# A gated decoder pair on one core: the feed-forward's down projection in three reduced products, the keys stacked in two parts, and a weight sum moved into the channel attention

## What is computed

```python
x = x + tanh(g_xattn[0]) * L0_xattn(layernorm(x), ctx, ctx)   # channel attention, sigmoid scores
x = x + tanh(g_ffn[0]) * L0_ffn(layernorm(x), ...)
x = x + tanh(g_xattn[1]) * L1_xattn(layernorm(x), ctx, mask, ...)  # 16 heads, 8-bit linears
x = x + tanh(g_ffn[1]) * L1_ffn(layernorm(x), W1, W2)         # ternary weights

def L0_ffn(x, w_r, b_r, w1, b1, w2, b2):
    scores = x @ w_r + b_r
    _, idx = top_k(scores, 0.5 * 512 -> k rows per batch)      # the best half, 256 tokens
    h = gelu(x[idx] @ w1 + b1)                                 # 512 -> 2048
    out[idx] = h @ w2 + b2                                     # 2048 -> 512, zero elsewhere

def weight_quant(w):                                           # of L1_ffn, W1 and W2
    scale = 1.0 / clip(mean(abs(w)), 1e-5)
    return clip(round(w * scale), -1, 1) / scale
```

## Time and profile before

| what | value |
|---|---|
| time, median of 3 runs | 994.96 us (993.64 to 995.98) |
| the profiled execution, its own time | 996.59 us |
| its span in the trace | 994.8 us |
| PE busy, share of the span | 893.2 us, 90% |
| DVE busy | 678.7 us, 68% |
| ACT busy | 573.3 us, 58% |
| mean granted TensorE clock | 0.978 of full speed |

### The profile page before, as it was taken

One profiled execution on the slowest core, in us unless ns is written; L12 is line 12 of the kernel. 1 busy time (PEld: TensorE's weight loads), 2 busy tenths in 40 slices (PEclk: granted clock), 3 DMA queues, 4 the chain that ended last, 5 costly groups with the idle time before them and its releaser, 6 DMA issues.

```text
span 994.8 us, 15838 instructions
## 1 busy us (share of the span) xinstructions
PE 893.2 (90%) x5584; PEld 585.3 (59%) x5592; DVE 678.7 (68%) x1893; ACT 573.3 (58%) x1098; POOL 81.9 (8%) x101
## 2 busy tenths in 40 slices
PE   3989998999999978699899999899999899899677
PEld 2868775576776654466544567544566545566333
DVE  5896762525222054599788699788699788699793
ACT  4546333445555133488638688548688548688443
POOL 2000203022120002400010000010000010000000
PEclk9999999999999989799999999999999999999879
DMA  5444556533351056910159310159410159300001
GB/s 190 131 166 135 193 218 232 176 129 128 103 194 43 1 169 148 192 43 2 44 107 199 118 43 2 44 108 192 124 43 2 43 108 198 118 1 2 1 1 43
DMA packets 52271, 102.83 MB, mean 103 GB/s; under 512 B 8925, under 2 KB 8925, under 8 KB 50657
## 3 DMA queue, kind: packets, MB, share of 16 engines
q1 hardware_dynamic: 39872, 71.88, 27.4%
q10 hardware_dynamic: 8160, 17.31, 5.2%
q0 software_dynamic: 4160, 12.62, 4.0%
HBM read 55.62 MB, written 14.75 MB: 71 GB/s over the span
## 4 chain that ended last, share of the span: by engine, by line
PE 39%; DVE 7%; issue 6%; ACT 6%; SPq 3%; DMA 3%; POOL 1%; ACTq 0%; DVEq 0%; POOLq 0%
PE psum L1518 8%; PE psum L1486 6%; PE psum L1535 5%; PE psum L1591 5%; PE psum L1561 5%; ACT probs L1334 3%; SPq L1187 3%; PE psum L1453 3%; DMA k<-k_lo 2%; PE psum L1463 2%; PE psum L1577 1%; PE psum L1544 1%; POOL q L1171 1%; DMA q<-first_parts 1%; PE psum L1479 1%
## 5 line engine op out<-in xcount | busy, mean ns | idle before, releaser
L1334 ACT ACTIVATE probs<-psum,neg_max 128x512 f32<-128x512 f32 x256 | 174.7, 691 | 47.3 <-DVE neg_max L1802 47.1
L1802 DVE CUSTOM_DVE_ANT_0 psum<-psum,m_in 128x512 f32<-128x512 f32 x256 | 174.3, 705 | 22.2 <-issue 22.1
L1518 PE MATMUL psum<-ident,probs 128*128 128x128 f32 x1024 | 154.0, 275 | 0.0
L1486 PE MATMUL psum<-k,q 128*128 128x512 f32 x256 | 125.4, 495 | 15.7 <-ACT probs L1334 7.3
L1518 PEld LDWEIGHTS psum<-ident,probs 128*128 128x128 f32 x1024 | 127.7, 141 | 19.6 <-issue 2.0
L674 PE MATMUL psum<-w_sb,hT 128*128 128x512 f32 x256 | 117.3, 603 | 5.9 <-ACT hT L566 5.9
L1832 DVE COPY probsT<-psum 128x512 f32<-128x512 f32 x128 | 88.1, 688 | 4.1 <-PE psum L1518 2.8
L1325 ACT COPY probsT<-psum 128x512 f32<-128x512 f32 x128 | 75.2, 588 | 20.9 <-PE psum L1518 20.9
L594 PE MATMUL psum<-xselT_hi,w_hi 128*128 128x256 f32 x256 | 81.8, 320 | 1.6 <-ACT xselT_hi L501 1.6
L1486 PEld LDWEIGHTS psum<-k,q 128*128 128x128 f32 x256 | 49.0, 192 | 53.1 <-ACT probs L1334 33.4
L674 PEld LDWEIGHTS psum<-w_sb,hT 128*128 128x128 f32 x256 | 46.9, 192 | 55.6 <-issue 48.2
(11 more groups left out here) (237 smaller groups left out, 1524.1 us busy)
## 6 DMA issues: line engine op xcount, KB each, us to landing
bw_raw<-in_L_ffn_W_dram ACTq DMA_DIRECT2D x16, 1024.0 KB, 5.4
c_in<-in_ctx_dram SPq DMA_DIRECT2D x8, 1024.0 KB, 5.3
k<-k_hi SPq DMA_DIRECT2D x24, 256.0 KB, 6.0
k<-k_lo SPq DMA_DIRECT2D x24, 256.0 KB, 6.8
q<-q_hi SPq DMA_DIRECT2D x48, 128.0 KB, 3.4
q<-q_lo SPq DMA_DIRECT2D x48, 128.0 KB, 2.5
xres<-in_x_dram SPq DMA_DIRECT2D x4, 1024.0 KB, 5.9
w_raw<-in_L_ffn_w_dram POOLq DMA_DIRECT2D x4, 1024.0 KB, 5.3
```

The source lines that it names most:

```text
L1334: act.activation(probs[:, u % 4, :], psum[u % SCORE_BANKS][:, :], ACT.Exp, scale=-1.0, bias=neg_max[:, u:u + 1], accum_out=prob_sum[:, nt, ...
L1486: pe.matmul(psum[u % SCORE_BANKS][:, :], q4[:, h, nt * P:(nt + 1) * P], k4[:, h, :], start=True, stop=True).then_inc(score_psum, 1)
L1518: mm = pe.transpose(turn_bank(u)[:, l * P:(l + 1) * P], probs[:, u % 4, l * P:(l + 1) * P], ident[:, :])
L1802: dve.tensor_tensor_reduce(bank[:, :], bank[:, :], m_in[:, nt, :], -1.0, LOWEST, ALU.add, ALU.min, neg_max[:, u:u + 1]).then_inc(masked_re ...
```

## The change

- The down projection uses `three` on high and low parts: 12 fp32r matmuls of 512 columns a pair in place of 4 fp32 ones. ACT adds a copy to `h_hi` per pair (`hidden_high`), DVE a subtraction to `h_lo` (`hidden_low`), in a ring of 3 buffers. `down(g)` runs two pairs behind `up`.
- `w2` is no longer resident as fp32. Its high part stays (`w2_hi`, made by ACT in the first 8 pairs and ahead of them). The raw rows go through a ring of 3 pair buffers, and every pair of every batch is loaded again (32 loads of 512 KB on SP) for DVE to make `w2_lo`. A slot is loaded again when `down` of three pairs before has been done.
- The ring lies on `xres` slots 1 and 2. So the order of batches is 0, 3, 1, 2 (`ORDER`): 3 is still in memory, 1 and 2 are read back from DRAM by SP (`load_x1`).
- The sums of magnitudes move into the channel attention: 3, 3 and 2 chunks at the end of batches 0, 1, 2 on ACT, ahead of the copies to `w1_hi`, through two buffers (`load_sum`) on the upper half of `w1_hi`. `FIRST_TURN` goes from 11 to 8, and the scales of both weights are made on DVE in the third pair.
- `load_selected` moves from SP to POOL. Ranks are made in two steps, in pairs 3 and 4; `route_norm` and `scores` in pairs 0 and 1, and the result of a batch is added in pair 1 of the next.
- The last `put_back` moves from the end of the first block to the head of the second. The rounding of wq and wo is spread over the pairs of the last batch; wk and wv are waited for in `layer1`.
- Keys of batches 1 to 3 are stacked in two halves (32 DMAs of 128 KB), the first as soon as two key tiles have both parts.

The core of the diff, left out lines marked:

```diff
+        RING = 3
+        ORDER = [0] + [B - 1] + list(range(1, B - 1))
...
+        w2_hi = at("w2_hi", [P, FT, C], F32R, w2_at)
+        w2_raw = at("w2_raw", [P, 2 * RING, C], F32, sh.front + 8 * K)
+        w2_lo = at("w2_lo", [P, 2 * RING, C], F32R, sh.front + 8 * K)
...
+                def load_selected(k):
+                    pool.wait_ge(xn_sel_stored, 16 * T * (k + 1))
+                    if k >= 1:
+                        pool.wait_ge(xsel_psum, 2 * k)
+                        pool.wait_ge(ids_ready, k)
+                    else:
+                        pool.wait_ge(sig_psum, B * CT_)
+                    pool.dma_start(xn_sel[:, :, :], sel_dram[k].rearrange("(j p) c -> p j c", p=P)).then_inc(xn_sel_loaded, 16)
...
-                put_back(B - 1)
...
+                def load_w2(g):
+                    k, p = divmod(g, PAIRS)
+                    if g >= RING:
+                        k0, p0 = divmod(g - RING, PAIRS)
+                        if p0 == PAIRS - 1:
+                            sp.wait_ge(osel_psum, (k0 + 1) * JT)
+                        else:
+                            sp.wait_ge(w2_used, k0 * (PAIRS - 1) + p0 + 1)
+                    i = g % RING
+                    sp.dma_start(w2_raw[:, 2 * i:2 * i + 2, :], w2[2 * P * p:2 * P * (p + 1), :].rearrange("(f p) c -> p f c", p=P)
+                                 ).then_inc(w2_loaded[i], 16)
+                def load_x1(k):
+                    sp.wait_ge(xnr_ready, k * T)
+                    sp.dma_start(xres[:, 0, :, :], tiles(sh.x_mid[ORDER[k]])).then_inc(x1_loaded, 16)
...
+                for g in range(RING, B * PAIRS):
+                    load_w2(g)
+                    k, p = divmod(g, PAIRS)
+                    if p == 3 and k + 2 < B:
+                        load_x1(k + 2)
+                    if g == (B - 2) * PAIRS + 3:
+                        sp.wait_ge(xnr_ready, B * T)
+                        load_weight(0, wq, wq_loaded)
+                    if g == (B - 1) * PAIRS:
+                        sp.wait_ge(xn_sel_stored, 16 * T * B)
+                        load_weight(3, wo, wo_loaded)
+                sp.wait_ge(w2_used, (B - 1) * (PAIRS - 1) + PAIRS - 2)
+                load_weight(2, wk, sh.wk_loaded)
+                sp.wait_ge(osel_psum, B * JT)
+                load_weight(1, wv, sh.wv_loaded)
...
+                def load_sum(n):
+                    dst, src = chunk(*divmod(n, 4), sum_raw[n % 2])
+                    act.dma_start(dst, src).then_inc(sum_loaded[n % 2], 16)
+                def magnitude(n):
+                    act.wait_ge(sum_loaded[n % 2], 16 * (n // 2 + 1))
+                    act.activation(sum_raw[n % 2][:, :], sum_raw[n % 2][:, :], ACT.Abs,
+                                   accum_out=bw_part[:, n // 4, n % 4:n % 4 + 1]).then_inc(magnitude_ready, 1)
+                    act.wait_ge(magnitude_ready, n + 1)
+                    if n + 2 < 8:
+                        load_sum(n + 2)
...
+                        for n in range(3 * b, min(3 * b + 3, 8)):
+                            magnitude(n)
...
+                def w2_high(g):
+                    act.wait_ge(w2_loaded[g % RING], 16 * (g // RING) + 16)
+                    if g == PAIRS - 2:
+                        act.wait_ge(xn_sel_stored, 16 * T)
+                    i = g % RING
+                    act.copy(w2_hi[:, 2 * g:2 * g + 2, :], w2_raw[:, 2 * i:2 * i + 2, :]).then_inc(w2_hi_ready, 1)
...
+                def hidden_high(g):
+                    act.wait_ge(h_ready, 2 * g + 2)
+                    act.copy(h_hi[g % RING][:, :, :], h_raw[g % RING][:, :, :]).then_inc(h_hi_ready, 1)
...
+                def down(g):
+                    k, p = divmod(g, PAIRS)
+                    pe.wait_ge(h_lo_ready, g + 1)
+                    pe.wait_ge(w2_lo_ready, g + 1)
+                    if p == 0 and k:
+                        pe.wait_ge(x2_ready, k * JT)
+                    for i in range(2):
+                        f = 2 * p + i
                         for j in range(JT):
-                            mm = pe.matmul(psum[j][:, :], hT[:, f % RING, j * P:(j + 1) * P], w2_sb[:, f, :],
-                                           start=(f == 0), stop=(f == FT - 1))
+                            mm = three(psum[j][:, :], [h[g % RING][:, i, j * P:(j + 1) * P] for h in (h_hi, h_lo)],
+                                       [w2_hi[:, f, :], w2_lo[:, 2 * (g % RING) + i, :]], f == 0, f == FT - 1)
                             if f == FT - 1:
                                 mm.then_inc(osel_psum, 1)
+                    if p < PAIRS - 1:
+                        mm.then_inc(w2_used, 1)
...
+                for g in range(B * PAIRS):
+                    k, p = divmod(g, PAIRS)
+                    up(g)
+                    if k + 1 < B and p == PAIRS - 1:
+                        if k == 0:
+                            pe.wait_ge(bw_inv_ready, 2)
+                        turn_selected(k + 1)
+                    weights(g)
+                    if g >= 2:
+                        down(g - 2)
+                    if k + 1 < B and p == (2 if k else 3):
+                        spread_scores(k + 1, psum[4])
+                down(B * PAIRS - 2)
+                down(B * PAIRS - 1)
...
+                def w2_low(g):
+                    i = g % RING
+                    dve.wait_ge(w2_loaded[i], 16 * (g // RING) + 16)
+                    dve.wait_ge(w2_hi_ready, min(g + 1, PAIRS))
+                    f = 2 * (g % PAIRS)
+                    dve.tensor_tensor(w2_lo[:, 2 * i:2 * i + 2, :], w2_raw[:, 2 * i:2 * i + 2, :],
+                                      w2_hi[:, f:f + 2, :].bitcast(F32), ALU.subtract).then_inc(w2_lo_ready, 1)
+                def hidden_low(g):
+                    dve.wait_ge(h_hi_ready, g + 1)
+                    dve.tensor_tensor(h_lo[g % RING][:, :, :], h_raw[g % RING][:, :, :],
+                                      h_hi[g % RING][:, :, :].bitcast(F32), ALU.subtract).then_inc(h_lo_ready, 1)
...
+                def put_together(k):
+                    dve.wait_ge(x_sel_ready, k + 1)
+                    for j in range(JT):
+                        dve.wait_ge(osel_psum, k * JT + j + 1)
+                        dve.scalar_tensor_tensor(x_sel[k % 2][:, j, :], psum[j][:, :], gate_f0, x_sel[k % 2][:, j, :],
+                                                 ALU.mult, ALU.add).then_inc(x2_ready, 1)
+                def route_next(k, p, link):
+                    n = k + 1
+                    if p == 0:
+                        if n == 1:
+                            route_stats(link, n)
+                        route_norm(link, n)
+                    elif p == 1:
+                        scores(link, n)
+                    elif p == 2 and k == 0:
+                        w1_lows(range(6, PAIRS))
+                        for i in range(2):
+                            bw_unit(i)
+                    elif p == 3:
+                        ranks(link, n, range(2))
+                    elif p == 4:
+                        ranks(link, n, range(2, T))
                         assert link.count == CHAIN_B
-                        selected_lows(b + 1)
-                    else:
-                        whole_weights()
-                    dve.wait_ge(x_sel_ready, b + 1)
-                    for j in range(JT):
-                        dve.wait_ge(osel_psum, b * JT + j + 1)
-                        dve.scalar_tensor_tensor(x_sel[b % 2][:, j, :], psum[j][:, :], gate_f0, x_sel[b % 2][:, j, :],
-                                                 ALU.mult, ALU.add).then_inc(x2_ready, 1)
+                    elif p == PAIRS - 1:
+                        selected_lows(n)
...
+                for g in range(B * PAIRS):
+                    k, p = divmod(g, PAIRS)
+                    hidden_low(g)
+                    if k and p == 1:
+                        put_together(k - 1)
+                    if g == 1:
+                        w2_low(2)
+                    if k + 1 < B:
+                        route_next(k, p, link)
+                        if p == PAIRS - 1 and k + 2 < B:
+                            link = Link(dve, chain_b, CHAIN_B, k + 2)
+                            route_stats(link, k + 2)
+                        elif p == PAIRS - 1:
+                            link = Link(dve, chain_w, 0, 0)
+                    else:
+                        round_next(p, link)
+                    if g >= RING:
+                        w2_low(g)
+                put_together(B - 1)
...
+                for j in range(sh.ids.shape[2]):
+                    pool.indirect_dma_start(
+                        sh.x_mid[sh.last_batch][:, :], bass.IndirectOffsetOnAxis(ap=sh.ids[:, B - 1, j:j + 1], axis=0),
+                        sh.x_sel_last[:, j, :], None).then_inc(sh.x2_stored[sh.last_batch], 16)
...
+                    for half in range(2):
+                        sp.wait_ge(k_hi_ready, b * CT_ + 2 * half + 2)
```

(8 more changed lines are left out.)

311 lines of the change are left out of this document (142 added, 169 removed).

## The result

The changed kernel takes **980.12 us** (median of four runs, 978.90 to 981.98) against 995.47 for the kernel before on the same chip (993.64 to 996.32): ratio 0.9848, 95% interval [0.9835, 0.9861]. It is faster, as forecast, but by 15 us and not by 25; the time lies 0.1 us outside the range.

What follows compares the result with a forecast made beforehand. PE was taken to bound the feed-forward, busy 55.00 of 55.00 us. Feed-forward -26.7, channel attention +4.3, block edge -1.7 and keys -0.5 sum to -24.6, giving about 970 us, range 959 to 980.

Steps and rivals of the forecast that it cites:

- Down projection: Feed-forward: twelve three-term matmuls take 2.72 us a pair in place of 3.48, over 32 pairs -24.3 us.
- First batch: Feed-forward's first batch: PE's 5.9 us of waits for hT go; new waits, from the order inside DVE, add 4.5.
- from a last rank to loaded rows takes 7.6 us: First feed-forward batch: with 0.3 to 0.5 more for POOL's queue, rows meet turn_selected about 1.8 us late.
- the +1.0 for the other batches: Other feed-forward batches: routing begins a slot or more earlier relative to PE, leaving 0.5 us at two spreadings of scores.
- Chunk chain: ACT's weight chunks take 11.5 us against two slots of 12.0: +0.5; as rival, landing in 7.5 gives +10, 980, chance 0.10.
- w2's ring: Feed-forward rival: reloading w2's three buffers sets the pace, the kernel gets slower than before, 1018 us; chance 0.05.
- POOL's: Rival: POOL is held up with scatters and row loads, 3 us more on each of three batches, +8: 978; chance 0.07.
- Channel attention: Magnitude sums moved there cost +4.3 us: +3.0 waiting for the residual at the edge to batch 2, +1.3 before rows load.
- without the scatter DVE is last: -1.7: Edge of the blocks: DVE ended at 348.06, POOL's last scatter at 349.79, so moving the scatter gains 1.7 us.
- before the mask load's wait on SP: free: Head of the second block: the moved scatter, 2.2 us first in POOL's queue, costs nothing.
- wv has 10 us: Edge of the blocks: wv's load starts there and has 10 us.
- Keys: Second block: stacking keys in halves removes ACT's 2.2 us wait, mostly hidden by PE: -0.5 us for three batches.

Runs made afterwards that it cites:

- keys_whole: Changed kernel with keys stacked in one part of 16 copies, as before the change: 981.69 us, ratio 0.9868.
- before_k_low: Kernel before the change, with only the low part of the second layer's first key tile made ahead of the rounding: 995.58 us against 994.76, ratio 1.0008.
- wv_early: Changed kernel with wv loaded three slots earlier, into another, already free weight buffer: 978.96 us, ratio 0.9833.
- chunk_early: Changed kernel with the first 1 MB chunk of ternary weights loaded three slots earlier: 979.74 us, ratio 0.9844.
- four_edits: Changed kernel with the edits of chunk_early, wv_early, scatter_late and k_low_first together: 968.00 us, ratio 0.9729.
- chunk_late: Changed kernel with the first chunk of the second layer's magnitudes loaded one slot later: 975.31 us, ratio 0.9795.
- late_wv_early: Changed kernel with first chunk three slots earlier, wv 30 us earlier, last scatter after c_in and x_in: 974.66 us, ratio 0.9804.
- late_four: four_edits with the first chunk loaded one slot later than in the changed kernel, not three earlier: 967.39 us, ratio 0.9734.
- scatter_in_first: Changed kernel with the last scatter issued at the end of the first layer again: 984.06 us, ratio 0.9876.
- scatter_late: Changed kernel with the last scatter, still in the second layer, issued only after c_in and x_in have landed: 985.19 us, ratio 0.9877.
- k_low_first: Changed kernel with DVE making the low part of the second layer's first key tile ahead of the rounding: 976.97 us, ratio 0.9821.
- five_edits: four_edits with the eight magnitude sums spread 2, 3 and 3 over the first three attention batches, not 3, 3 and 2: 970.37 us, ratio 0.9757.

## Why the prediction came out as it did

**Down projection.** The mechanism was right, the size off by 3.2 us: the row promised 2.72 a pair, and it took 2.78, or 2.86 next to turned blocks (16 x 0.06 + 16 x 0.14), -21.1 and not -24.3. Counted from slot to slot it is the same: 6.78 became 6.15 with turned blocks. The ratio of the two forms is 0.80. The Trainium skill (FP8 and Floating Point Precision, TensorE Precision Notes) has true fp32 as four passes, and three for four would take a quarter off, 0.87 a pair. 0.70 and 0.62 came, so the measured row was the better guide, and even it was a little too good.

**First batch.** The 5.9 us of waits went, as forecast. The new ones were forecast as 0.4, 0.7, 1.6 and 1.8 and came as 0, 0.64, 1.16 and 5.53. The last is the step that failed: "from a last rank to loaded rows takes 7.6 us". It took 13.2 (from 160.97 to 174.13). With 7.6 the rows would have met PE, which stood from 168.69 on, without a wait. Two things were wrong with the step. The pace was the shortest of four in the trace: the later batches of the kernel before took 8.5 to 9.8. And no load stood ahead of the rows there (three of w2 were issued 0.4 us behind them), while the change itself put a megabyte 1.6 us ahead, in the slot that I had counted as ahead of use; without it the load takes 4.8 us and not 8.0. The wait of 3.1 us for the scatters, on POOL now and on SP before, is not new: there it was 1.7 to 4.2. With the slow clock behind the stall (below) the step cost 5.4 us more than the forecast had for it. The three smaller waits gave 0.9 back, and the +1.0 for the other batches did not come.

**Chunk chain, w2's ring, pace.** PE waited 1.1 us for turned blocks, 0.5 forecast, and never for w2's parts. The rivals that made a ring or a chain the pace did not come; POOL's did in one place of three, by a longer landing of the load, not by slower instructions.

**Channel attention.** +4.0 against +4.3 (+3.0 to +5.4 over the kernels with the same attention): the wait for the residual is 6.55, forecast about 7.1, and PE waits 0.88 for the first rows, forecast 1.3. The third chunk of an edge came as reckoned, ACT waited 5.00 us for it, until 47.84 (forecast 47). Taking the sums out gives 2.7 of it back.

**Edge.** The step "without the scatter DVE is last: -1.7" saw only the 1.7 us of POOL's issuing. The 3.6 us behind it were the scatter's too. The edge gave 4.9.

**Entry.** The step that failed is "before the mask load's wait on SP: free" with "wv has 10 us". I asked who waits for the scatter and for wv, not what their bytes do to the load beside them. `x_in` landed 3.8 us later relative to the block, and a chain of DVE and SP's 16 and then 32 copies handed all of it on, to the first scores or to the ninth unit, plus the low clock: 6.7 us in the profiled execution and 4 at least in the others, where 0 was forecast. Of the 3.8 us, 2.8 are the scatter and wv together; where the last 1.0 comes from is open. The edge's -4.9 and this +6.7 make +1.8, or -0.9 with the loss of 4.0: the move of the scatter and of wv gave nothing that can be told.

**Keys.** Forecast -0.5 for three batches. The mechanism was right: ACT's wait went, and keys_whole puts it at 0.3 us in each of batches 1 and 2, so some 0.9 if batch 0 gives as much. Batches 1 to 3 are 2.0 shorter, but most of that is not the change: 1.4 lies in the last batch, where no keys are stacked, and before_k_low, the same code as the kernel before from there on, has 437.7 us in place of 439.6. That the table's row is larger than forecast is luck.

## What to carry to other kernels

When a transfer is moved to a place where nobody waits for it, ask what lands beside it: here two moved transfers made a third one 3.8 us late, and the loss came out 60 us further on, at another engine. When a pace is read from a trace, look at every place where the step occurs: the one row used here was the shortest of four. A wait that goes when its cause is taken away may leave the sum as it was (wv_early); test the sum of the stages, not the stage. And where one engine's queue stands ahead of a long chain of copies, the order inside that queue is worth more than the transfers' own timing.

## What the runs showed of the hardware

- **The clock after a stall.** After the stalls of 4.3 (wv_early), 5.5 and 6.5 us the granted clock is 0.5, that is 1.2 in place of 2.4 GHz, for some 3 to 7 us once work begins again. After stalls of 2.3 to 3.1 us it goes either way: low after 2.48 (chunk_early), 2.53 (four_edits), 2.83 (changed kernel) and 3.09 (chunk_late), full after 2.27 (late_wv_early), 2.91 (late_four) and the 2.50 at 343.42 (changed kernel). The two kernels with full clock behind their wait for the second batch's rows have the shortest feed-forwards of those with three terms, 199.3 and 199.6 us. After the 5.53 us at 174.22 the next eight turns took 1.59 us and not 0.88, the next `down` 3.75 and not 2.78: 1.7 us on top of the stall. In the window with the 2.83 us before 406.77 the mean clock was 0.66. The forecast priced stalls by their length alone.
- **Spread between kernels that share a stage.** The feed-forward of layer0 is the same code in seven of the kernels (but for the place of wv's load in one); in their profiles it takes 203.7 to 205.1 us in five, 210.3 in scatter_in_first and 212.5 in scatter_late, where PE waited 3.2 us for ACT's turned blocks at 260.86 and 1.7 at the head of a batch. Totals of one kernel also spread by 10 us (k_low_first: 971.95 to 982.51), those of the kernel before by 5. five_edits spreads by 12, four_edits and late_four by 4. That loads which are met just in time make this spread is how I read the waits, and was not tried.
- **A block's end waits for its last scatter to land**: 3.6 and 6.3 us after POOL had issued it.
